# Half as many query/key projection matmuls in a decoder layer: two heads in one stationary operand, keys ahead of queries, denominators from a column of ones

## The reference

```python
q = einsum('bxy,iyk->bxik', x, Wq).reshape(h, b, t, hs)   # k and v alike
wei = where(causal, einsum('hbqd,hbkd->hbqk', q, k) * hs ** -0.5, -inf)
out = einsum('hbqk,hbkd->hbqd', softmax(wei, axis=-1), v).reshape(b, t, h * hs)
x = layernorm(x + out @ proj_w.T + proj_b)
x = layernorm(x + cross_attention(x, ctx, ctx, mask))      # softmax over 77 context rows
x = layernorm(x + experts(x))
```

## Time and profile before

| | |
|---|---|
| time, median of 3 runs | 2056.43 us (2056.19 to 2057.38) |
| the profiled execution | 2061.44 us, span 2058.4 us |
| mean granted PE clock | 0.928 of full speed |
| PE busy 0 to 40 us | none (weights are loaded and split) |
| attention block | 40 to about 1400 us |
| routing, experts, final norm | about 1400 to 2058 us |

### The profile page before, as it was taken

How to read it: one execution, slowest core, us unless ns; L and a number is a source line. 1 busy time by engine, 2 the same in 40 slices (tenths; PEclk the granted TensorE clock), 3 DMA queues, 4 the chain that set the end, 5 groups by cost and what they waited for, 6 DMA issues and landing times. The chain is left out here.

```text
span 2058.4 us, 63859 instructions
## 1 busy us (share of the span) xinstructions
PE 1672.2 (81%) x21906; PEld 1483.1 (72%) x21907; DVE 1255.8 (61%) x2999; ACT 1066.6 (52%) x3094; POOL 783.3 (38%) x1054
## 2 busy tenths in 40 slices
PE   2888889888888888898888888861799999999920
PEld 1788778778777787787877877740788888888820
DVE  4577767677676677677766777646734334333347
ACT  4566666667666666676666666520033333333324
POOL 1133335344443453444433533320144444444411
PEclk9999999999999999999999999855599999999975
DMA  5332222232223222322232211007211111111135
GB/s 142 113 110 89 86 67 68 72 100 77 70 74 98 78 68 65 97 87 70 63 98 88 68 52 47 22 6 322 86 39 36 37 36 36 39 36 38 38 122 208
DMA packets 139465, 162.02 MB, mean 79 GB/s; under 512 B 78334, under 2 KB 110206, under 8 KB 136832
## 3 DMA queue, kind: packets, MB, share of 16 engines
q1 hardware_dynamic: 128128, 136.94, 20.5%
q0 software_dynamic: 6912, 17.84, 2.8%
q10 hardware_dynamic: 4224, 4.19, 0.6%
HBM read 93.92 MB, written 66.06 MB: 78 GB/s over the span
## 5 line engine op out<-in xcount | busy, mean ns | idle before, releaser
L1364 ACT ACTIVATE act_g<-ps_e,b 128x128 f32<-128x128 f32 x576 | 164.7, 369 | 313.3 <-PE ps_e L1327 290.6
L1327 PE MATMUL ps_e<-xt,wres 128*128 128x128 f16 x3456 | 260.8, 218 | 2.8 <-issue 2.6
L1327 PEld LDWEIGHTS ps_e<-xt,wres 128*128 x3456 | 234.4, 97 | 24.4 <-issue 6.3
L877 POOL TENSOR_TENSOR o_st<-o_norm,o_st 128x256 f16<-128x256 f32 x128 | 85.8, 671 | 380.8 <-ACT o_st L590 380.8
L578 ACT ACTIVATE probs<-ps,nbias 128x128 f32<-128x128 f32 (+1 forms) x512 | 211.0, 417 | 8.4
L1385 DVE SCALAR_TENSOR_TENSOR e_y<-ps_e,b 128x256 f32<-128x256 f32 x72 | 30.6, 425 | 292.7 <-PE ps_e L1338 292.7
L1289 POOL DMA_INDIRECT z_scr<-e_y,rows_out x72 | 130.0, 1805 | 204.2 <-DVE e_y L1385 199.1
L1338 PE MATMUL ps_e<-wres,g_hi 128*128 x1152 | 192.8, 272 | 10.5 <-issue 4.3
L382 PE MATMUL ps<-x_hi,w_q 128*128 128x128 f16 x2048 | 196.9, 222 | 3.5 <-issue 3.2
L382 PE MATMUL ps<-x_hi,w_k 128*128 128x128 f16 x2048 | 187.2, 219 | 0.2
L382 PE MATMUL ps<-x_lo,w_q 128*128 128x128 f16 x1024 | 182.3, 222 | 0.0
(11 more groups left out here) (259 smaller groups left out, 4813.6 us busy)
## 6 DMA issues: line engine op xcount, KB each, us to landing
piece<-in_moe_w SPq DMA_DIRECT2D x24, 768.0 KB, 6.5
w_scr<-piece_pair SPq DMA_DIRECT2D x24, 768.0 KB, 4.1
wres<-w_scr SPq DMA_DIRECT2D x18, 1024.0 KB, 22.2
v_scr<-v_tok SPq DMA_DIRECT2D x32, 512.0 KB, 2.6
v_pos<-v_scr SPq DMA_DIRECT2D x32, 512.0 KB, 4.3
z_scr<-zero SPq DMA_DIRECT2D x32, 256.0 KB, 3.8
f_z<-z_scr SPq DMA_DIRECT2D x8, 1024.0 KB, 5.6
x_t<-in_xT SPq DMA_DIRECT2D x32, 128.0 KB, 6.1
```

Of the source, the lines that this page charges most:

```text
L1327: last = mm(out, w(b, c * FF + f * P, P), xt[:, p, a, c], start=(m == 0), stop=(m == 5))
L1364: nc.scalar.activation(act_g[:, p, f], ps[:, 3 + 2 * p + f // 4, (f % 4) * P:(f % 4 + 1) * P], ACT.Gelu, bias=bias[:, f:f + 1], scale=1.0 ...
```

## The change

A query or key fill now takes two different heads in one stationary operand: head h on partitions 0 to 63, head h + 8 on 64 to 127, so a fill of four 128-column blocks has eight heads, and a tile has two fills of each kind. ACT and DVE evacuate a fill in two halves of 64 partitions. The low part of queries goes to partitions 64 to 127 of `q_st`; the keys, high and low, are written to partitions 0 to 63 of `k_pair` and a DMA copies them to 64 to 127. Keys come ahead of queries. Fills: slot 0 v1, slot 3 k1, slot 5 q0, slot 6 q1, slot 7 v0 and k0 of the tile after next. The values get a column of ones in front (`v_pos`, `v2_hi`), the sum comes out of `pv` and `pv2` as one more column, and its reciprocal is taken in `normalise` and at slot 0 of D. `accum_out`, `invert`, `sums`, `q_hi` and `lo_rows` go.

```diff
@@ -43,10 +43,16 @@
-FILLS = [("v", 0), ("q", 0), ("v", 1), ("q", 1), ("q", 2), ("q", 3), ("k", 0), ("k", 1), ("k", 2), ("k", 3)]
+FILLS = [("v", 0), ("k", 0), ("v", 1), ("k", 1), ("q", 0), ("q", 1)]
 NF = len(FILLS)
-V_FILLS = 3
-FILLS_OF_SLOT = [[2, 3], [], [4], [5], [6, 7], [8], [9], []]
+PAIRS = H // 2
+
+
+OPS_BEFORE = [sum(1 if kind == "v" else 2 for kind, _ in FILLS[:j]) for j in range(NF + 1)]
+NOPS = OPS_BEFORE[NF]
+V_OPS = OPS_BEFORE[3]
+K_OPS = OPS_BEFORE[4]
+FILLS_OF_SLOT = [[2], [], [], [3], [], [4], [5], []]
@@ -122,9 +127,9 @@
         for n in "qk":
-            for copy in range(2):
-                pairs.append((ld[n], 16, stage[n][:].rearrange("p c (h d) -> p c h d", d=HS),
-                              [wqk[n][:, k, :, :, copy, :] for k in range(2)], WA_UP))
+            for a in range(2):
+                pairs.append((ld[n], 16, stage[n][:, :, a * PAIRS * HS:(a + 1) * PAIRS * HS].rearrange("p c (h d) -> p c h d", d=HS),
+                              [wqk[n][:, k, :, :, a, :] for k in range(2)], WA_UP))
         pairs.append((ld["v"], 16, stage["v"][:], [wv[:, k] for k in range(2)], WA_UP))
@@ -181,16 +183,13 @@
     x_lo = sb("x_lo", [P, 2, KC, P], F16)
-    q_hi = sb("q_hi", [P, 2, P, 4], F16)
     q_st = sb("q_st", [P, 2, P, H], F16)
-    k_hi = sb("k_hi", [P, 2, P, H], F16)
-    k_lo = sb("k_lo", [P, 2, P, H], F16)
+    k_pair = sb("k_pair", [P, 2, 2, P, H], F16)
     v_tok = sb("v_tok", [P, 2, H, 2, HS], F16)
-    v_pos = sb("v_pos", [P, 2, 2 * GROUPS, 2, HS], F16)
+    v_pos = sb("v_pos", [P, 2, 2 * GROUPS, 1 + 2 * HS], F16)
     nmax = sb("nmax", [P, 2], F32)
...
     probs = sb("probs", [P, 384], F32)
-    den = sb("den", [P, 2, 4], F32)
     rden = sb("rden", [P, 4], F32)
@@ -302,9 +303,9 @@
                 t = s + 1
-                sp.wait_ge(s_fill_hi, NF * t + V_FILLS)
+                sp.wait_ge(s_fill_hi, NOPS * t + V_OPS)
                 sp.sem_inc(s_held_sp, 1)
-                sp.wait_ge(s_fill_lo, NF * t + V_FILLS)
+                sp.wait_ge(s_fill_lo, NOPS * t + V_OPS)
                 sp.sem_inc(s_held_sp, 1)
@@ -315,7 +316,9 @@
                     sp.sem_inc(s_held_sp, 1)
-                sp.dma_start(v_pos[:, q].rearrange("p g k d -> p g (k d)"),
+                if isinstance(s, int) and s == -1:
+                    sp.wait_ge(s_one, 2)
+                sp.dma_start(v_pos[:, q, :, 1:1 + 2 * HS],
                              io["v_scr"][q].rearrange("(g t) (h e) -> (t h) g e", t=GTOK // 2, h=H)).then_inc(s_v_in, 16)
@@ -335,6 +338,11 @@
                     sp.dma_start(z[:, n:n + 2 * D], zero[:]).then_inc(s_z_out, 16)
+            if "A" in stages:
+                t = s + 1
+                sp.wait_ge(s_fill_lo, NOPS * t + K_OPS)
+                sp.sem_inc(s_held_sp, 1)
+                sp.dma_start(k_pair[HS:P, q], k_pair[0:HS, q]).then_inc(s_kdup, 16)
             if "D" in stages:
@@ -366,7 +374,7 @@
             if since(t, 1) or j >= 2:
-                pe.wait_ge(s_fill_lo, NF * t + j - 1)
+                pe.wait_ge(s_fill_lo, NOPS * t + (OPS_BEFORE[j - 1] if j else OPS_BEFORE[NF - 1] - NOPS))
             bank = ps_a[j % 2]
@@ -374,21 +382,22 @@
             else:
-                for hh in range(4):
-                    h = 4 * n + hh
+                for i in range(4):
                     w = wqk[kind]
...
                     for m, (a, b, c) in enumerate(steps_):
-                        last = mm(bank[:, hh * P:(hh + 1) * P], w[:, b, c, h].rearrange("p k d -> p (k d)"), xs[a][:, c],
+                        last = mm(bank[:, i * P:(i + 1) * P], w[:, b, c, 4 * n + i].rearrange("p k d -> p (k d)"), xs[a][:, c],
                                   start=(m == 0), stop=(m == 5))
...
             if g == 0:
-                pe.wait_ge(s_fill_lo, NF * (t + 1))
+                pe.wait_ge(s_fill_lo, NOPS * (t + 1))
+                pe.wait_ge(s_kdup, 16 * (t + 1))
             if since(t, 1) or g:
                 pe.wait_ge(s_exp, 2 * (GROUPS * t + g))
-            qs, kh, kl = (m[:, p, g * GTOK:(g + 1) * GTOK].rearrange("p t h -> p (t h)") for m in (q_st, k_hi, k_lo))
+            qs, kh, kl = (m[:, g * GTOK:(g + 1) * GTOK].rearrange("p t h -> p (t h)")
+                          for m in (q_st[:, p], k_pair[:, p, 0], k_pair[:, p, 1]))
             mm(ps_s[:, 0:P], qs[:, 0:P], kh[:, 0:P], start=True, stop=False, skip_group_check=True)
@@ -412,11 +421,17 @@
             for q in range(2):
-                out = ps_o[:, (g % 2 * 2 + q) * HS:(g % 2 * 2 + q + 1) * HS]
+                at = (g % 2 * 2 + q) * (1 + HS)
                 blocks = [(0, 0)] if q == 0 else [(1, 0), (2, 1)]
...
                 for m, (a, b, blk, c) in enumerate(todo):
-                    last = mm(out, a[:, blk * P:(blk + 1) * P], v_pos[:, p, 2 * g + c, b], start=(m == 0), stop=(m == len(todo) - 1))
+                    v = v_pos[:, p, 2 * g + c]
+                    if b == 0:
+                        last = mm(ps_o[:, at:at + 1 + HS], a[:, blk * P:(blk + 1) * P], v[:, 0:1 + HS], start=(m == 0),
+                                  stop=(m == len(todo) - 1), skip_group_check=True)
+                    else:
+                        last = mm(ps_o[:, at + 1:at + 1 + HS], a[:, blk * P:(blk + 1) * P], v[:, 1 + HS:1 + 2 * HS], start=False,
+                                  stop=False, skip_group_check=True)
             last.then_inc(s_pv, 1)
@@ -488,8 +503,10 @@
                 h = HB * cc + n
-                for m, (a, b) in enumerate(((pt2_hi, 0), (pt2_lo, 0), (pt2_hi, 1))):
-                    last = mm(c7[:, h * DK:(h + 1) * DK], a[:, n], v2[:, b, h * DK:(h + 1) * DK], start=(m == 0), stop=(m == 2))
+                at = h * (1 + DK)
+                mm(c7[:, at:at + 1 + DK], pt2_hi[:, n], v2_hi[:, h], start=True, stop=False, skip_group_check=True)
+                mm(c7[:, at + 1:at + 1 + DK], pt2_hi[:, n], v2_lo[:, h], start=False, stop=False, skip_group_check=True)
+                last = mm(c7[:, at:at + 1 + DK], pt2_lo[:, n], v2_hi[:, h], start=False, stop=True, skip_group_check=True)
             last.then_inc(s_pv2, 1)
@@ -557,17 +574,13 @@
             if kind == "v":
-                src = ps_a[j % 2].rearrange("p (h d) -> p h d", d=HS)
-                dst = v_tok[:, p, 8 * n:8 * n + 8, 0]
-            elif kind == "q":
-                if since(t, 1) or j >= 3:
-                    act.wait_ge(s_fill_lo, NF * t + j - 1)
-                src = ps_a[j % 2].rearrange("p (h t) -> p t h", h=4)
-                dst = q_hi[:, j % 2]
-            else:
-                src = ps_a[j % 2].rearrange("p (h t) -> p t h", h=4)
-                dst = k_hi[:, p, :, 4 * n:4 * n + 4]
-            nc.scalar.activation(dst, src, ACT.Copy).then_inc(s_fill_hi, 1)
+                nc.scalar.activation(v_tok[:, p, 8 * n:8 * n + 8, 0], ps_a[j % 2].rearrange("p (h d) -> p h d", d=HS),
+                                     ACT.Copy).then_inc(s_fill_hi, 1)
+                return
+            to = q_st[:, p] if kind == "q" else k_pair[:, p, 0]
+            for a in range(2):
+                src = ps_a[j % 2][a * HS:(a + 1) * HS].rearrange("p (h t) -> p t h", h=4)
+                nc.scalar.activation(to[0:HS, :, PAIRS * a + 4 * n:PAIRS * a + 4 * n + 4], src, ACT.Copy).then_inc(s_fill_hi, 1)
@@ -575,8 +588,8 @@
             for q, (lo_, up_) in enumerate(((0, P), (P, 384))):
-                nc.scalar.activation(probs[:, lo_:up_], ps_s[:, lo_:up_], ACT.Exp, bias=nbias[:, q:q + 1], scale=SCORE_SCALE,
-                                     accum_out=den[:, g // 2 % 2, g % 2 * 2 + q:g % 2 * 2 + q + 1]).then_inc(s_exp, 1)
+                nc.scalar.activation(probs[:, lo_:up_], ps_s[:, lo_:up_], ACT.Exp, bias=nbias[:, q:q + 1],
+                                     scale=SCORE_SCALE).then_inc(s_exp, 1)
@@ -592,7 +605,7 @@
             if since(t, 1) or cc:
-                act.wait_ge(s_den2, 2 * t + cc)
+                act.wait_ge(s_t2, 4 * t + 2 * cc)
             nc.scalar.activation(probs2[:], sm_shift[:], ACT.Exp, scale=SCORE2_SCALE).then_inc(s_exp2, 1)
@@ -671,20 +686,19 @@
             kind, n = FILLS[j]
-            dve.wait_ge(s_fill_hi, NF * t + j + 1)
             if kind == "v":
+                dve.wait_ge(s_fill_hi, NOPS * t + OPS_BEFORE[j] + 1)
                 src = ps_a[j % 2].rearrange("p (h d) -> p h d", d=HS)
...
                     op0=ALU.mult, op1=ALU.subtract).then_inc(s_fill_lo, 1)
-            elif kind == "q":
-                src = ps_a[j % 2].rearrange("p (h t) -> p t h", h=4)
-                stt(out=q_st[:, p, :, 4 * n:4 * n + 4], in0=q_hi[:, j % 2], scalar=lo_rows[:, 0:1],
-                    in1=src, op0=ALU.mult, op1=ALU.add).then_inc(s_fill_lo, 1)
-            else:
-                src = ps_a[j % 2].rearrange("p (h t) -> p t h", h=4)
-                at = (slice(None), p, slice(None), slice(4 * n, 4 * n + 4))
-                stt(out=k_lo[at], in0=src, scalar=1.0, in1=k_hi[at],
-                    op0=ALU.mult, op1=ALU.subtract).then_inc(s_fill_lo, 1)
```

(29 more changed lines are left out.)

36 lines of the change are left out of this document (18 added, 18 removed).

## The result

The changed kernel takes 2043.76 us (median of 4 runs, 2042.11 to 2046.04), the one before 2056.31 (4 runs beside it, 2056.09 to 2057.38). The ratio is 0.9937, 95% interval 0.9923 to 0.9951: 12.6 us faster, where I forecast 31. The time lies in my range, and under half of the gain came.

The account below looks back on a forecast made before the run. A loop of waits through all engines, not PE, was taken as the bound. Loop -20, unrolled steps -4, first tile -5, steps 0 and 1 -3, last -1: -33, giving 2023 for the runs; forecast 2025 us, range 1972 to 2064.

Parts of the forecast that it names:

- What bounds the kernel: Whole step: a loop of waits through all engines is the limit, not PE work; PE's share falls to about 75%.
- The key copy: New 512 KB DMA after `k1`, 4.3 us to landing: hidden in the steps, some 3 us in the first tile.
- The first tile, steps 0 and 1: Kernel start: six fills at about 1.75 us against ten at 1.95, plus the copy: -5 us; the two steps -3.
- The step's sum: One step: shifts of its stations after less before, the projection at 0, ending with the next projection at -0.8 us.
- `predicated` 0: The `predicated` of the first half in a step: forecast to shift by -0.1 us.
- maxima 7: Maxima of group 7 in a step: -0.4 us, from two accumulator pairs less and PE no longer late.
- `predicated` 1: The `predicated` of the second half: +0.25 us, from the second half of `q1`, the reciprocal and fewer accumulators.
- end of the low parts: Where a step's low parts end: +0.6 us, from the second half of `k0` on ACT, then DVE.
- the hold as a rival: DVE copies starting at partition 64 lose their overlap: 1.0 us a step on the chain, 2048 us; chance 0.2.
- The loop's turn: PE stands 3.5 us unexplained, then is later in slot 0, where the 1.34 us fill counts: this step -0.9 us.
- The ones column: Denominators: accumulators 0.18 us a group, two DVE sums 0.70 each in queue, reciprocal +0.2; the column itself costs nothing.
- The clock: Rival: PE idles to half clock once a step, 1.8 us each, +56, 2079 us; sign under 0.95; chance 0.2.

Follow-up runs that it names:

- the ones column alone: Kernel before with only the denominators changed (ones column in the values, no accumulators or row sums), its ten fills kept: 1968.7 us with the attention loop unrolled, 2030.1 in the loop.
- before written out: Kernel before with the 12 turns of its attention loop written as 24 steps in a row, same work: 2010.0 us, ratio 0.9769.
- the runs written out: Kernels with the 12 turns of the attention loop as 24 steps in a row: the one before 2010.0 us, the changed one 2028.4.
- the kernel with the added wait: Changed kernel, loop as 24 steps, both VectorE low halves of a fill waiting for ScalarE's second high half: 2115.2 us; with ScalarE's high halves at partition 0, 2090.9.
- the pair projection alone: Changed kernel with the old denominators (accumulators, row sums, no ones column), its six fills kept: 2062.3 us with the loop as 24 steps, 2090.8 in the loop.
- the kernel with its fills placed otherwise: Changed kernel, loop as 24 steps, query fills late in slots 4 and 5, none in slot 6, both slot 7 fills ahead of the scores: 2021.2 us.

## Why the prediction was wrong in its sum, and where it was right

*What bounds the kernel.* Right. PE lost the forecast matmuls (75% share, as said) and the time hardly moved.

*The key copy.* Hidden in the steps, as said: PE waited for it once, in the first tile. But there it waited 5.63 us where I had 3; this copy, issued at 50.09, took 8.1 us to land, the others 4.6 in the median:

```profile
58.33 0.27 PE L401 MATMUL ps<-k_pair,q_st 128*128 128x128 f16 x1 [5.63 <-DMA k_pair<-k_pair]
```

*The first tile, steps 0 and 1.* Forecast -5 and -3; measured -0.4 at the first maxima (59.4 against 59.8) and +6.5 by step 5. The six fills took from 39.75 to 51.24, where the next tile's first fill begins: 1.9 us each and not 1.75; that seventh fill ends at 52.70, and there the wait for the copy begins. In steps 0 and 1 PE then waits at the product with the values for `o_norm`, which waits on VectorE:

```profile
71.23 0.21 PE L430 MATMUL ps<-v_pos,pt_hi 128*128 128x65 f16 x1 [1.82 <-DVE o_norm L721]
79.87 0.19 PE L430 MATMUL ps<-v_pos,pt_hi 128*128 128x65 f16 x1 [2.40 <-DVE o_norm L721]
```

With the ones column alone, `y` of step 2 starts 2.1 us sooner than in before written out (135.70 against 137.75), so it is the pair projection that loses here. Which of its operations does was not tested. The clock is one candidate: after the wait for the copy, PE works at half clock for more than half of the stretch that follows. Windows of after, then of before:

```profile
56.00:84.00 28.00, 19.51 (x186) 16.95 (x187) 11.53 (x29) 13.19 (x34) 3.87 (x6) 0.70 0.49 147
```

```profile
56.00:84.00 28.00, 24.44 (x337) 21.15 (x335) 15.53 (x38) 17.39 (x55) 4.66 (x8) 0.94 0.39 127
```

This is the largest miss of the sum in us: +6.5 where I had -8, which is 14.5 of the 17 us between the 33 forecast and the 16.2 of the profiled executions (the ledger below).

*The step's sum.* Failed. Stations of the step shown above, from the start of the `bn_stats` on `y`, shift after less before: `predicated` 0 -0.02 (forecast -0.1), maxima 7 -0.15 (-0.4), `predicated` 1 +0.68 (+0.25), end of the low parts +1.26 (+0.6), `o_norm` +0.39 (-0.2), the next step's `bn_stats` +0.67 (-0.8). Against the forecast each station down to the end of the low parts is later (by 0.1, 0.25, 0.4 and 0.7) by a term that I left out, about a hold more with every pair copy that was passed. The last one has a stretch at half clock on top (below). The step that failed is "each fill that stays now has two of each: +0.48 us in ACT's queue and +0.61 in DVE's": with the holds it is about 0.74 and 0.83 (1.22 and 1.44, less what one copy takes in the queue). I had named the hold as a rival, for VectorE alone and at 1.0 us a step, with a chance of 0.2. The runs give 0.79 us a step for VectorE and 0.76 for ScalarE (24.3 / 32, in the kernel with the added wait; 0.54 at equal clock). So the mechanism of the rival came true and twice over, and "no row shows a hold" was a reason from silence: no copy of before starts anywhere but at partition 0.

*The loop's turn.* Failed the other way. I gave the step that holds it -0.9, as if the stall of the earlier trace rows were a wait that lessens. It went altogether: the change takes 30.9 us from the cost of the loop (46.3 less 15.4), 2.6 a turn. A loop iteration became 2.0 us shorter (from `y` at 300.83 to 1128.88 before, 303.34 to 1111.72 after, ten turns), which is close to the -1.7 of my sum, by two errors that cancel: two steps 1.3 us longer in place of shorter, and a turn 3 us shorter. Without the runs written out the agreement would have passed for a confirmation.

*The ledger.* Between the two profiled executions (spans 2058.4 and 2042.2): start +6.5 (forecast -8), loop -23.0 (-20), unrolled full steps +0.7 (-4), last ones -2.3 (-1), the rest of the kernel +1.9 (0). In all -16.2, the medians say -12.6. Written out, by cause: ones column -41.3; pair projection +59.7, of which holds of VectorE 25.4 and of ScalarE 24.3. The last 10 us are not shown apart. By place, the 59.7 are 11.1 up to `y` of step 5, 43.1 from there to step 27 and 5.5 behind; of the 43.1, 35.3 are work of the steps (a pair at full clock takes 79.0 against 75.8 us) and 7.9 the eight slow steps. The open part may lie in the start, in the clock, or in the drain of a fill, which in the changed kernel takes from ScalarE's first half to the end of VectorE's second.

*The ones column.* Under-sized. My terms for it (accumulators 0.18 a group on the path, sums 0.70 twice in VectorE's queue, a reciprocal +0.2) came to a gain; its share was spread over stations and hidden by the projection's. Measured, it is worth 1.3 us a step.

*The clock.* I gave it a rival and put it at nothing in the sum. The rival's sign, an unrolled full step under 0.95, did not come (0.97 and 0.96), yet its mechanism did, in part. Two even steps of the changed kernel in the loop:

```profile
708.45:748.54 40.09, 31.22 (x428) 26.62 (x425) 28.67 (x69) 27.57 (x62) 17.93 (x25) 1.00 0.33 94
788.04:828.96 40.92, 32.44 (x428) 28.09 (x425) 28.76 (x70) 27.43 (x62) 17.85 (x25) 0.96 0.37 103
```

They are the same step, and the one with a stretch at half clock takes 0.83 us more. From step 5 to step 27, fifteen of 22 steps are of that sort, by 0.8 to 1.0 us each, 13.5 us; the rival had 1.8 us in every step. The stations above are of such a step, so 0.83 of the shift at the next `bn_stats` is the clock: in a step at full clock it would be about -0.15, not +0.67. The stretch begins at the start of a step without a turn:

```profile
820.36 1.47 PE L445 MATMUL ps<-ident,o_st 128*128 128x128 f16 x16 [0.98 <-POOL o_st L881]
822.13 0.88 PE L414 MATMUL ps<-ident,probs 128*128 128x128 f32 x3
```

One step earlier, at 781.53 and 782.71, the same transposes take 1.06 and 0.52 us. PE had 0.98 us idle right before; but two steps earlier, at 740.8, it had the same 0.98 us and kept its clock, so this wait alone does not decide.

The clock is also a part of the loop cost that has no stall (15 and 28 us). From `y` of step 5 to that of step 27 the changed kernel takes 888.8 us in the loop and 876.9 written out. Steps at full clock are 0.3 us longer in the loop (40.09 and 39.50 against 39.80 and 39.22), 6.5 us in 22; and fifteen slow steps in place of eight are 5.6 us. For the pair projection alone the same stretch takes 23.7 us more in the loop, and the time at half clock in it goes from 37 to 119 us. Why the clock falls more often in the loop, and what the 0.3 us are, stays open; no run holds the clock.

## What to carry to other kernels

Before a change is priced in a loop, look at the packets that load instructions and at idle time at the turn: here 46 us of 2056 were the loop, 35 of them a stall at its turn, a shorter body hid a change for the worse behind it, and writing the loop out was worth more than the change. The packets alone are no sign, since code written out loads them too (140 and 116) without a stall; packets and idle time at the turn together are. Compare steps at the same granted clock before a cause is named: here the clock was half of the loss in the steps, and it hid a gain of 1 us a step from the placement of the fills. Split a change with two parts and run each: one gained 41 us, the other lost 52 alone and 60 on top of it. When a copy is cut into halves that start at other partitions, price each half as a whole copy without overlap, on VectorE and on ScalarE, and count it where the step waits for the drain, whatever TensorE saves.

## What the runs showed of the hardware

- ScalarE, too, gives up the overlap of neighbouring instructions when the partitions at which they start change: a pair of 64x512 copies took 1.20 us and the next came at 1.22; all at partition 0, 1.07 and 0.98. With the pairs of ScalarE at partition 0 a kernel with 128 of them was 24.3 us faster, of which some 17 at equal clock (0.54 us a step).
- A loop whose body holds 826 matmuls on PE went round with 44 instruction packets in the whole execution; with 1018 there were 172, and PE stood 3.2 us a turn with nothing to wait for; with 1652, 126 packets in half as many turns, 3.0 us a turn on PE and 4.3 on VectorE.
- A wait of one VectorE copy for one ScalarE copy more, four times a step, cost 87 us, 2.5 us a step at full clock.
- One step of the changed kernel, the same work: 40.09 us at a granted clock of 1.00, 40.92 at 0.96; slot 6 to 7 of the kernel with its fills placed otherwise: 7.29 us at 1.00, 8.96 at 0.81.
